# Last stage of a two-layer kernel: plain loads of both sum arrays, variance by ScalarE, fewer shared units before the experts

## The reference, cut to what matters

```python
x = L0_attn_x                                   # (1, 4096, 512), float32
x = layernorm(x + linear_attention(x))          # decayed running sums over 16 heads
T, E, K, CAP = 4096, 64, 6, 128
scores = softmax(x @ gate_w.T)                  # 64 experts
topk_w, topk_idx = top_k(scores, 6)             # each expert keeps at most 128 tokens
routed = sum over experts of ((silu(g) * u) @ down_proj[e]) * weight, added to each token's row
shared = silu(x @ sg.T) * (x @ su.T) @ sd.T     # 512 -> 384 -> 512, every token
out = layernorm(x + routed + shared)            # eps 1e-5, variance over 512 values
```

## Time and profile before

| | us |
|---|---|
| median of 3 runs (lowest, highest) | 1085.03 (1084.44, 1088.70) |
| the profiled execution, its own time | 1084.22 |
| its span in the profile | 1082.4 |
| last scatter of the table to its load by SP | 592.7 to 593.9 |
| last expert's rows scaled, first unit of the last stage on ACT | 978.4, 981.2 |
| busy PE, PEld, DVE, ACT, POOL | 967.9, 765.2, 690.7, 488.2, 597.9 |

### The profile page before, as it was taken

How to read it: one execution, slowest core, us unless ns; L and a number is a source line. 1 busy time by engine, 2 the same in 40 slices (tenths; PEclk the granted TensorE clock), 3 DMA queues, 4 the chain that set the end, 5 groups by cost and what they waited for, 6 DMA issues and landing times.

```text
span 1082.4 us, 15024 instructions
## 1 busy us (share of the span) xinstructions
PE 967.9 (89%) x4578; PEld 765.2 (71%) x4578; DVE 690.7 (64%) x1159; ACT 488.2 (45%) x965; POOL 597.9 (55%) x614
## 2 busy tenths in 40 slices
PE   5899999898999989889999998999899899999453
PEld 4777878686877868678887766677676667777342
DVE  5977776768776776766443655566556565652785
ACT  4422434334243343424343555566565555652343
POOL 4324376858667675866466254445444454442674
PEclk9989999999999999989999999999999999999786
DMA  5352431535143243317241599999999999989996
GB/s 161 98 165 87 149 79 63 141 99 139 54 138 90 69 140 104 117 31 260 67 150 54 190 300 297 314 302 316 295 301 321 293 308 321 317 245 238 291 247 185
DMA packets 116670, 203.93 MB, mean 188 GB/s; under 512 B 19440, under 2 KB 59376, under 8 KB 115568
## 3 DMA queue, kind: packets, MB, share of 16 engines
q1 hardware_dynamic: 91888, 158.82, 45.1%
q0 software_dynamic: 24704, 44.16, 18.6%
HBM read 143.03 MB, written 59.90 MB: 187 GB/s over the span
## 4 chain that ended last, share of the span: by engine, by line
PE 25%; DMA 21%; issue 5%; POOL 4%; ACT 3%; DVE 1%; POOLq 0%; DVEq 0%; ACTq 0%; SPq 0%
PE bank L1322 22%; DMA xg<-x_rows,table_sb 10%; DMA acc_rows<-eo,table_sb 5%; DMA fin<-acc_rows 5%; PE bank L1484 2%; ACT wgu_hi L778 1%; POOL acc_rows L1284 1%; ACT eo L784 1%; POOL rstd L1219 1%; POOL slot_table L1253 1%; POOL shift L1221 0%; DVE stats L878 0%; PE bank L1521 0%; POOL rstd L1217 0%; POOL fin L1315 0%
## 5 line engine op out<-in xcount | busy, mean ns | idle before, releaser
L1253 POOL DMA_INDIRECT slot_table<-tokens,slot_of x192 | 205.7, 1071 | 64.9 <-issue 57.0
L1284 POOL DMA_INDIRECT acc_rows<-eo,table_sb x64 | 111.8, 1747 | 185.8 <-ACT eo L784 162.1
L1322 PE MATMUL bank<-x_hi,wqkv_hi 128*128 128x512 f32 x384 | 155.0, 404 | 12.4 <-DVE wqkv_lo L855 12.4
L1322 PE MATMUL bank<-x_hi,wqkv_lo 128*128 128x512 f32 x384 | 151.5, 395 | 0.0
L1322 PE MATMUL bank<-x_lo,wqkv_hi 128*128 128x512 f32 x384 | 151.3, 394 | 0.0
L1111 DVE TENSOR_TENSOR wgu_lo<-wgu,wgu_hi 128x1536 fp32r<-128x1536 f32 x64 | 112.4, 1758 | 45.0 <-ACT wgu_hi L778 45.0
L1322 PE MATMUL bank<-wdn,hid_et 96*128 96x512 f32 x256 | 121.3, 596 | 0.8 <-ACT hid_et L821 0.8
L1245 POOL TENSOR_TENSOR num<-phi_q,run_kv 128x512 f32<-128x512 f32 x32 | 55.3, 1727 | 96.7 <-DVE phi_q L1056 96.6
L778 ACT CAST wgu_hi<-wgu 128x1536 fp32r<-128x1536 f32 x64 | 94.3, 1475 | 1.8 <-DMA wgu<-w_gu 1.8
L1322 PEld LDWEIGHTS bank<-x_hi,wqkv_hi 128*128 128x128 f32 x384 | 73.3, 191 | 28.1 <-DVE wqkv_lo L855 14.1
L1322 PE MATMUL bank<-wgu_hi,xgt_hi 128*128 128x384 f32 x256 | 91.6, 358 | 0.0
(11 more groups left out here) (149 smaller groups left out, 2283.7 us busy)
## 6 DMA issues: line engine op xcount, KB each, us to landing
wgu<-w_gu SPq DMA_DIRECT2D x64, 768.0 KB, 8.3
wdn<-w_down SPq DMA_DIRECT2D x64, 384.0 KB, 7.9
xres<-x SPq DMA_DIRECT2D x32, 256.0 KB, 3.3
acc_rows<-zeros SPq DMA_DIRECT2D x8, 1024.0 KB
x_turned<-x1t SPq DMA_DIRECT2D x32, 256.0 KB, 3.6
x_rows<-x SPq DMA_DIRECT2D x32, 256.0 KB, 3.3
acc_rows<-x SPq DMA_DIRECT2D x32, 256.0 KB, 3.4
x1t_stage<-x_turned SPq DMA_DIRECT2D x8, 1024.0 KB
```

The source lines that it names most:

```text
L1253: pool.indirect_dma_start(table_dram, bass.IndirectOffsetOnAxis(slot_of[:, i, k:k + 1], 0), tokens[:, i:i + 1], None, bounds_check=SLOTS - ...
L1284: pool.indirect_dma_start(acc_dram[e % 2], bass.IndirectOffsetOnAxis(table_sb[:, e:e + 1], 0), eo[eo_slot[e]][:, :], None, bounds_check=T ...
L1322: mm = pe.matmul(out_ap, a, b, start=first and i == 0, stop=final and i == len(products) - 1)
```

## The change

- The nine last steps hold 16 units in place of 25: the middle place of a step is empty, and the last two steps lose their first one. With the six units that follow, 22 units stand ahead of the experts in place of 31; 18 are in the experts (17 before), and 24 in the last stage (16 before), which now holds three shared blocks. Shared rows of five blocks are kept.
- On ACT and DVE, three of the six units stand ahead of the waits for the scatters and stores.
- The turned rows of blocks 1 to 7 are loaded by DMAs on ACT's queue, behind the first tanh of the block ahead; they were on SP's.
- In the last stage both arrays are loaded by plain DMAs on SP, into a ring of 5 buffers `fin` and one of 4 buffers `odd`. SP waits for all scatter-adds of both arrays first (it waited for all of the even and all but one of the odd ones). Four blocks are loaded at once, the others when a buffer is free.
- For each tile, DVE now adds the odd sums, then adds the shared rows and sums each row in the same instruction (`accum_out`). POOL makes the negative mean of it, ACT the sum of squares of the row less its mean (`Square`, `accum_out`), POOL rstd and shift by three operations, and ACT applies them two tiles later. `bn_stats` and `bn_aggr` are gone here.

```diff
-    TAIL = 2
+    TAIL = 3
...
+    FRING = 8
+    fin_sum, fin_mean, fin_square, fin_rstd, fin_shift = [both.place(f"fin_{s}", [P, FRING])
+                                                          for s in ("sum", "mean", "square", "rstd", "shift")]
...
-    fin_map = Map(nc, late_weights_at, fin_end)
-    fin_sb += [fin_map.place(f"fin{i}", [P, NJ, D]) for i in range(2, NB)]
-    FINS = len(fin_sb)
+    fin_map = Map(nc, late_weights_at, end)
+    NFA, NFB = 5, 4
+    fin_sb += [fin_map.place(f"fin{i}", [P, NJ, D]) for i in range(2, NFA)]
+    odd_sb = [fin_map.place(f"odd{i}", [P, NJ, D]) for i in range(NFB)]
+    squares = [Map(nc, x_at + 2 * half - 4 * D, x_at + 2 * half).place("squares0", [P, D]),
+               Map(nc, x_at + 4 * half - 4 * D, x_at + 4 * half).place("squares1", [P, D])]
...
-        return it >= NB, (it == NB and c > 0) or it == NB + 1, it >= NB
+        return NB <= it and (it, c) < (NB + 1, 3), False, it >= NB
...
+    block_order = sorted(range(NB), key=lambda b: fin_no[b, 0])
+    fin_place = {b: m for m, b in enumerate(block_order)}
+
+    def last_fin(m):
+        return fin_no[block_order[m], NJ - 1]
+
+    def loads_behind(n):
+
+        return [m for m in range(NFB, NB)
+                if n == max(last_fin(m - NFB), last_fin(m - NFA) if m >= NFA else 0)]
...
-            def load_x1t(b):
-                sp.wait_ge(q_mm, KC * (NB - 1))
-                last_tile = b * NJ + NJ - 1
-                for lane in range(2):
-                    sp.wait_ge(x1t_out[lane], 16 * ((last_tile - 1 + lane) // 2 + 1))
-                if b:
-                    sp.wait_ge(x1t_lo_done, KC * b)
-                sp.dma_start(x1t_stage[:, :, :], x1t_dram[b]).then_inc(x1t_in, 16)
...
+            def load_sums(m):
+                b = block_order[m]
+                rows = slice(b * BT, (b + 1) * BT)
+                if m >= NFB:
+                    sp.wait_ge(fin_joined, last_fin(m - NFB) + 1)
+                if m >= NFA:
+                    sp.wait_ge(fin_out[m % NFA], 16 * NJ // 2 * (m // NFA))
+                sp.dma_start(fin_sb[m % NFA][:, :, :], acc_dram[0][rows, :].rearrange("(j p) d -> p j d", p=P)).then_inc(fin_in[m % NFA], 16)
+                sp.dma_start(odd_sb[m % NFB][:, :, :], acc_dram[1][rows, :].rearrange("(j p) d -> p j d", p=P)).then_inc(odd_in[m % NFB], 16)
...
+            sp.wait_ge(eo_done, NE)
+            sp.wait_ge(rows_added[0], 16 * NE // 2)
+            sp.wait_ge(rows_added[1], 16 * NE // 2)
+            for m in range(NFB):
+                load_sums(m)
...
+                for m in loads_behind(n):
+                    load_sums(m)
...
+            def load_x1t(b):
+                last_tile = b * NJ + NJ - 1
+                for lane in range(2):
+                    act.wait_ge(x1t_out[lane], 16 * ((last_tile - 1 + lane) // 2 + 1))
+                act.wait_ge(x1t_lo_done, KC * b)
+                act.dma_start(x1t_stage[:, :, :], x1t_dram[b]).then_inc(x1t_in, 16)
...
+                        if part == 0 and b + 1 < NB:
+                            load_x1t(b + 1)
...
+            for _ in range(BEFORE_EXPERTS[0]):
+                unit()
             act.wait_ge(rest_mm, NT)
             act.wait_ge(out_mm, NT)
             act.wait_ge(slot_done, NT)
...
+            def square_tile(n):
+                i = n % FRING
+                act.wait_ge(fin_mean_done, n + 1)
+                if n >= 2:
+                    act.wait_ge(fin_squared, n - 1)
+                act.activation(squares[n % 2][:, :], fin_rows(n), ACT.Square, bias=fin_mean[:, i:i + 1],
+                               accum_out=fin_square[:, i:i + 1]).then_inc(fin_squared, 1)
...
+            def apply_tile(n):
+                i = n % FRING
+                act.wait_ge(fin_shift_done, n + 1)
+                act.activation(fin_rows(n), fin_rows(n), ACT.Identity, bias=fin_shift[:, i:i + 1],
+                               scale=fin_rstd[:, i:i + 1]).then_inc(fin_applied, 1)
...
+                if 1 <= n <= NFIN:
+                    square_tile(n - 1)
+                if n >= 3:
+                    apply_tile(n - 3)
...
-                dve.wait_ge(fin_merged[fin_slot[b]], 16)
+                m, i = fin_place[b], n % FRING
+                z = fin_sb[m % NFA][:, j, :]
+                dve.wait_ge(fin_in[m % NFA], 16 * (m // NFA + 1))
+                dve.wait_ge(odd_in[m % NFB], 16 * (m // NFB + 1))
+                dve.tensor_tensor(z, odd_sb[m % NFB][:, j, :], z, ALU.add).then_inc(fin_joined, 1)
                 if b < EARLY:
                     dve.wait_ge(rows_copied, NJ * b + j + 1)
-                    dve.tensor_tensor(z, shared_rows[b][:, j, :], z, ALU.add).then_inc(fin_added, 1)
+                    shared = shared_rows[b][:, j, :]
                 else:
                     dve.wait_ge(down_mm, NJ * b + j + 1)
-                    dve.tensor_tensor(z, proj_ps[rows_take[b, j] % 3][:, :], z, ALU.add).then_inc(fin_added, 1)
-                dve.wait_ge(fin_added, n + 1)
-                norm(NT + n, z)
+                    shared = proj_ps[rows_take[b, j] % 3][:, :]
+                dve.wait_ge(fin_joined, n + 1)
+                if n >= FRING:
+                    dve.wait_ge(fin_applied, n - FRING + 1)
+                dve.scalar_tensor_tensor(out=z, in0=shared, scalar=1.0, in1=z, op0=ALU.mult, op1=ALU.add,
+                                         accum_out=fin_sum[:, i:i + 1]).then_inc(fin_added, 1)
...
+            for _ in range(BEFORE_EXPERTS[0]):
+                unit()
             dve.wait_ge(rest_mm, NT)
             dve.wait_ge(out_mm, NT)
             dve.wait_ge(score_done, NT)
...
+            def mean_of(n):
+                i = n % FRING
+                pool.wait_ge(fin_added, n + 1)
+                pool.tensor_scalar(fin_mean[:, i:i + 1], fin_sum[:, i:i + 1], -1.0 / D, None, ALU.mult).then_inc(fin_mean_done, 1)
...
+            def rstd_of(n):
+                i = n % FRING
+                at = slice(i, i + 1)
+                pool.wait_ge(fin_squared, n + 1)
+                pool.tensor_scalar(fin_rstd[:, at], fin_square[:, at], 1.0 / D, EPS_NORM, ALU.mult, ALU.add).then_inc(fin_var_done, 1)
+                pool.wait_ge(fin_var_done, n + 1)
+                pool.tensor_tensor(fin_rstd[:, at], fin_rstd[:, at], minus_half[:, :], ALU.pow).then_inc(fin_rstd_done, 1)
+                pool.wait_ge(fin_rstd_done, n + 1)
+                pool.tensor_tensor(fin_shift[:, at], fin_mean[:, at], fin_rstd[:, at], ALU.mult).then_inc(fin_shift_done, 1)
...
-                while merged < NB and first_fin[block_order[merged]] <= n + MERGE_AHEAD:
-                    b = block_order[merged]
-                    merged += 1
-                    pool.wait_ge(fin_in[fin_slot[b]], 16)
-                    src = acc_dram[1][b * BT:(b + 1) * BT, :].rearrange("(j p) d -> p j d", p=P)
-                    pool.dma_start(fin_sb[fin_slot[b]][:, :, :], src, accum_op=ALU.add).then_inc(fin_merged[fin_slot[b]], 16)
-                norm(NT + n)
+                mean_of(n)
+                if n >= 2:
+                    rstd_of(n - 2)
```

112 lines of the change are left out of this document (27 added, 85 removed).

## The result

The changed kernel takes 1073.14 us (median of 20 runs, 1068.51 to 1084.59), the kernel before 1082.76 (20 runs): ratio 0.9908, 95% interval 0.9889 to 0.9928. That is about 10 us, where 23 were forecast, and the time lies just above the range's upper end of 1073. The profiled execution took 1071.41 us with a span of 1069.7.

The account below looks back on a forecast made before the run. PE and POOL together were taken to bound the steps, DMA the experts, accumulating DMAs and their followers the end. Steps -16, first rows -1, experts 0, last stage -6 gave -23 on 1084.2; median 1062 us, range 1053 to 1073.

Parts of the forecast that it names:

- Both come before POOL has issued the scatters queued ahead of them, but for 1 or 2 us: Last steps: output products for two norms arrive early enough that POOL hardly waits; last scatter at 577, -16 us.
- Rival 2: Last steps gain half: chain latency, not PE, feeds POOL; -8 in place of -16, total 1070; chance 0.10.
- First rows and sixth unit, -1: Ahead of the experts: sixth unit becomes a projection, -1.4, low-clock matmuls cost at most 2.4; taken -1 (+1 to -2).
- experts, 0: Experts: same bytes at the same rate, one unit more hidden behind full DMA engines; 0 us (0 to +4).
- Last stage, data: Last stage: all 26.2 MB takes 73 us, first loads arrive before DVE asks, the 27.8 us of data waits go.
- Rival 3: Last stage: DMA still bounds the end, 26.2 MB at 289 GB/s; S + 101, total 1065; chance 0.06.
- Last stage, DVE: S + 85.4: DVE's work, 67.0 us after S + 18.4, ends 85.4 us after S, the last stage's start.
- Last stage, ACT: 1.81 us a tile: Last stage: ACT's square, read and apply take 1.81 us per tile, 57.9 for 32, ending at S + 88.
- +3 to the longer of the two: Last stage: 3 us added to ACT's S + 88 for DVE and ACT delaying each other: S + 91, end S + 98.
- Rival 1: Last stage gains nothing: DVE's two-operand SBUF additions hold POOL, ACT waits for the mean; S + 105, total 1069; chance 0.16.
- Rival 4: Last stage: PE's clock falls to the low level; +44 there, in all +27, total 1111; chance 0.04.
- What would show it: Signs: gather near 580.5, PE bank waits not over 5 us; wrong if DVE waits over 10 us for ACT or sums.

Follow-up runs that it names:

- norm_behind: Changed kernel with POOL issuing a last step's six scatters ahead of that step's last norm instead of behind it; ratio 0.9810 against the kernel before.
- both_moves: Changed kernel with the edits of norm_behind and no_mean_op together; ratio 0.9770 against the kernel before, last stage 94.4 us.
- no_mean_op: Changed kernel with ACT squaring from the raw sum, scale -D, so POOL makes no mean, three operations a tile; ratio 0.9805 against before, last stage 95.1 us.
- mean_kept: no_mean_op with POOL's mean put back in its old place, its result awaited by nobody; ratio 0.9949 against the kernel before, last stage 112.2 us.
- mean_behind: no_mean_op with POOL's mean put back behind the square of its own tile; ratio 0.9840 against the kernel before, last stage 96.3 us.
- sets 1 and 2: First two of four groups of follow-up kernels, each with the kernel before on its own chip; before took 1094.17 and 1093.03 us there.
- sets 3 and 4: Last two of four groups of follow-up kernels, each with the kernel before on its own chip; before took 1081.67 and 1081.02 us there.
- more_lag: Changed kernel with ACT's square two tiles behind the additions, apply five, POOL's power three; ratio 0.9974 against the kernel before, last stage 111.3 us.

## Why the prediction was wrong

- **"Both come before POOL has issued the scatters queued ahead of them, but for 1 or 2 us".** This step failed, by 8 to 9 us. POOL's issue time of 79.6 was right within 2.2 us (87.4 less 10.0 of waits is 77.4), and so was the earliest end. What was wrong is that PE's saving reaches the norm whole: two products came 4.1 and 6.8 us earlier against the first scatter, where units of 8.2 and 11 us had been taken off PE. PE had a gap at last (it waited 1.62 us for DVE at 492.47, and its matmuls behind that started 0.43 us apart until 495.6, with a granted clock of 0.62 from 492.5 to 497.0), and the second product's statistics stood on DVE behind a low part that waited 4.21 us for ACT, which waited for POOL. Rival 2, with the tile's own chain through three engines and -8, describes what happened: -8.8. norm_behind and both_moves show the part that runs through POOL: with the scatters ahead of the norm, 6 us of the waits are gone on a chip without gaps. PE's part was read from the timeline and not tested.
- **First rows and sixth unit, -1; experts, 0.** Together -2.1 in the trace, at the lower end of the bounds (-2 to +5). The experts' length scatters by up to 7 us between executions of the same code, which the forecast had not allowed for.
- **Last stage, data.** Right: first addition at S + 18.4 without a wait, as said; 2.9 us of data waits in all. Rival 3 did not come.
- **Last stage, DVE: S + 85.4.** Right as a sum, wrong as a bound of the changed kernel. no_mean_op's last addition starts at S + 87.8 (counting S as the prediction does) and ends at 88.5; the 32 accumulator reads of 0.08, taken as 0, are 2.6 us of the difference. The changed kernel's ended at S + 97.4, outside the 85 to 92 given.
- **Last stage, ACT: 1.81 us a tile.** Too much: ACT goes at 1.41 a tile when it waits for nothing (square and apply at 0.72 and 0.81 overlap with the read). The square's own time was not the trouble.
- **Last stage, "+3 to the longer of the two".** This is the second step that failed, and the larger one: the stage took 3.4 us more than before in place of 6 less. It took ACT and DVE to share delays and left out POOL, as if it followed for free. POOL's mean of tile n stands ahead of root and shift of tile n - 2 in POOL's order and waits for DVE; with DVE's holds POOL needs up to 2.6 us a tile in a burst. The chain cost 9 us at DVE's last tile (97.4 against 88.5) and, with ACT six tiles behind there, 10 us in place of 7 to the end. no_mean_op, mean_kept and mean_behind show it: the order of POOL's operations alone is worth 10 us or more, their number about 1.
- **Rival 1** had the mechanism in part (POOL held, ACT waiting for the mean, S + 105 against 107.4) and the price nearly. The argument against it, that eight slots of statistics buffer it, fails because slots don't help an engine that works in order. What it lacked is that the hold costs little where the order makes no ring.
- **Rival 4.** The clock was 0.89 in the last stage, just under the 0.9 given; over stretches of 10 us in which PE had work it was 0.79 to 1.00. It did not come.
- **What would show it.** Two signs told of the failure: PE waited 6.0 us for a bank, and DVE over 10 us for ACT even without the 7.0 of the first unit (9.1 for tanh, 6.8 for high parts). The sign that seemed to come true, S 16.1 us earlier, did so by luck: 5.3 us of it lie ahead of the change.

The changed kernel with the two failed steps mended (both_moves) has a ratio of 0.9770; the forecast's 1062 over 1085.03 was 0.9788. A gain of that size was there, in another order of instructions. That the two numbers agree so well is partly luck, since the last stage then gains 9 us where 6 were forecast. It is luck too that the changed kernel's 1073.14 us come so near to the range: the kernel before was at 1082.76 in 20 runs, 2.3 us under the median that the forecast started from.

## What to carry to other kernels

When an engine issues in order, ask for each wait what stands behind it that is ready: here a mean of 0.2 us, placed ahead of three operations that were ready, cost at least 10 us, and six ready scatters behind a norm cost 6 us in the steps on one chip and 13 in all on another. Count the small operations on a third engine as part of the loop between two busy ones, at their length beside those engines' work. Run both halves of a change alone before believing either: each half was slower than before here, the whole faster, on two chips of the same kind of slowness. And a later consumer frees a buffer later: more slack for one wait can be a data wait at the next load.

## What the runs showed of the hardware

- On two of the chips, those of sets 1 and 2, ACT and DVE stood still for 2 to 9.5 us at a time with no engine or DMA in the trace to release them, in the kernel before too (5.38 us on DVE, above), and the kernel before took 1% longer there. No trace of sets 3 and 4, nor the first two, has such a gap. What they are was not found.
- An operation on one column took GpSimd 0.19 to 0.57 us alone, and up to 0.7 (root 1.09 in more_lag, shift 1.29 in mean_kept) beside VectorE instructions with two SBUF operands; that shift ended with the second of two of them.
- VectorE's accumulated sum cost a read of 0.08 us a tile; ScalarE's square with its read (0.72 and 0.19) and an apply of 0.81 fit in 1.41 us in no_mean_op, less than their sum of 1.72.
